# A Flamingo block with routed experts on one core: chunk sizes in another order, GpSimd's indirect DMAs released by other products and one at a time, and DVE's work moved between its maxima

## What is computed

```python
Q = split(layernorm(x) @ wq.T); K = split(ctx @ wk.T); V = split(ctx @ wv.T)
attn = softmax(einsum('bhqd,bhkd->bhqk', Q, K) / sqrt(8))
x = x + tanh(g_xattn) * merge(attn @ V)
y = layernorm(x)
logits = y @ Wr + br                       # 8 experts
topv, topi = top_k(logits, 2)
gates = softmax(where(chosen, logits, -inf))
h = relu(einsum('btd,edh->bteh', y, W1) + b1)
out = einsum('bte,bteh,ehd->btd', gates, h, W2) + einsum('bte,ed->btd', gates, b2)
x = x + tanh(g_ffn) * out
```

## Time and profile before

| | |
|---|---|
| median of 3 runs | 747.68 us (745.53 to 752.26) |
| the profiled execution's own time | 750.96 us |
| its span, first to last instruction | 749.2 us |
| PE busy with products | 601.1 us (80%) |
| DVE, ACT, POOL busy | 373.1, 368.3, 264.6 us |
| mean granted clock of TensorE | 0.88 of full speed |
| indirect DMAs issued by GpSimd | 112 scatters, 112 gathers |

### The profile page before, as it was taken

One profiled execution on the slowest core, in us unless ns is written; L12 is line 12 of the kernel. 1 busy time (PEld: TensorE's weight loads), 2 busy tenths in 40 slices (PEclk: granted clock), 3 DMA queues, 4 the chain that ended last, 5 costly groups with the idle time before them and its releaser, 6 DMA issues.

```text
span 749.2 us, 18488 instructions
## 1 busy us (share of the span) xinstructions
PE 601.1 (80%) x6213; PEld 430.1 (57%) x6213; DVE 373.1 (50%) x1361; ACT 368.3 (49%) x835; POOL 264.6 (35%) x281
## 2 busy tenths in 40 slices
PE   2459898868899887889989888988886679779467
PEld 0225555545566664556766557766455668667346
DVE  2446777765776445666544674454444032122044
ACT  5126755544566654456555555565553345344112
POOL 5020101045100345540444353444555661642720
PEclk9958988987999998799999889999798779999769
DMA  4445653554557524375644366632423435532211
GB/s 111 118 102 142 150 133 80 130 156 107 126 115 110 136 68 137 75 131 83 151 114 131 69 127 99 137 84 76 95 51 95 119 92 126 102 98 76 68 35 43
DMA packets 158121, 78.65 MB, mean 105 GB/s; under 512 B 85088, under 2 KB 153312, under 8 KB 158032
## 3 DMA queue, kind: packets, MB, share of 16 engines
q1 hardware_dynamic: 119760, 45.65, 28.6%
q10 hardware_dynamic: 31104, 17.13, 8.5%
q0 software_dynamic: 7168, 14.69, 7.6%
HBM read 30.72 MB, written 36.75 MB: 90 GB/s over the span
## 4 chain that ended last, share of the span: by engine, by line
PE 60%; issue 12%; DVE 10%; another core or an unknown queue 6%; ACT 6%; DMA 2%; ACTq 2%; SPq 1%; DVEq 0%
PE y L607 9%; PE scores L503 9%; PE bank_oT L517 9%; PE max_scores L482 5%; PE o L530 4%; PE hidden_p L593 3%; DVE neg_max L1025 3%; PE hidden_p L591 2%; ACT hidden L807 2%; PE max_scores L541 2%; PE bank_oT L647 2%; PE o L647 2%; PE hidden_p L592 2%; PE group L458 2%
## 5 line engine op out<-in xcount | busy, mean ns | idle before, releaser
L1025 DVE TENSOR_REDUCE neg_max<-max_scores 128x4 f32<-128x308 f32 x244 | 116.2, 476 | 177.6 <-PE max_scores L482 166.0
L741 ACT ACTIVATE probs<-scores 77x512 f32<-77x512 f32 x256 | 150.0, 596 | 88.5 <-PE scores L503 78.8
L1351 POOL DMA_INDIRECT back<-ys_dram,at x112 | 107.7, 961 | 110.3 <-PE scores L503 44.4
L1336 POOL DMA_INDIRECT xs_dram<-rows,at x112 | 109.5, 977 | 103.7 <-PE scores L503 75.3
L517 PE MATMUL bank_oT<-probs,v_cols 77*9 77x128 f32 x2048 | 112.2, 296 | 11.4 <-issue 6.3
L503 PE MATMUL scores<-q_st,k_st 128*77 128x128 bf16 x1024 | 115.3, 242 | 1.5 <-issue 1.3
L482 PE MATMUL max_scores<-k_st,q_st 128*128 128x308 bf16 x244 | 80.5, 330 | 41.0 <-DVE neg_max L1025 22.7
L503 PEld LDWEIGHTS scores<-q_st,k_st 128*77 128x77 bf16 x1024 | 79.3, 127 | 53.6 <-issue 46.1
L607 PE MATMUL y<-w_sb,hidden 128*128 x608 | 101.7, 314 | 0.0
L807 ACT ACTIVATE hidden<-hidden_p,b_cols 128x128 f32<-128x128 f32 x260 | 74.4, 370 | 50.3 <-PE hidden_p L593 40.8
L607 PEld LDWEIGHTS y<-w_sb,hidden 128*128 128x128 f32 x608 | 91.4, 216 | 3.3
(11 more groups left out here) (144 smaller groups left out, 943.3 us busy)
## 6 DMA issues: line engine op xcount, KB each, us to landing
ys_dram<-ys ACTq DMA_DIRECT2D x38, 256.0 KB
q_st<-q_dram SPq DMA_DIRECT2D x16, 512.0 KB
k_st<-k_dram SPq DMA_DIRECT2D x64, 77.0 KB
xs_all<-x SPq DMA_DIRECT2D x16, 256.0 KB, 3.9
q_dram<-q_hl SPq DMA_DIRECT2D x16, 256.0 KB
xs_dram<-zeros_b ACTq DMA_DIRECT2D x16, 256.0 KB, 3.2
out<-xs_all SPq DMA_DIRECT2D x16, 256.0 KB
k_dram<-k_hl SPq DMA_DIRECT2D x48, 77.0 KB
```

The lines of the kernel that those rows point to most:

```text
L741: nc.scalar.activation(probs[h][:], score_bank[h % 2][0:KEYS, :], ACT.Exp, scale=SCALE).then_inc(s_exp, 1)
L1025: V.tensor_reduce(neg_max[:, i // 2, :, h, i % 2], max_to(b, h)[:, 0:PER * KEYS].rearrange("p (j k) -> p j k", j=PER), AXIS_X, ALU.max, ne ...
L1336: G.indirect_dma_start(out=xs_dram[c % 2], out_offset=bass.IndirectOffsetOnAxis(ap=at[k][c % 4][:, i:i + 1], axis=0), in_=rows[c % 2][:, i ...
L1351: G.indirect_dma_start(out=back[k][:, b % 16, :], out_offset=None, in_=ys_dram[c % 2][0:TILES[c] * 128, :], in_offset=bass.IndirectOffsetO ...
```

## The change

The chunks become 12, 12, 12, 12, 8 sequences. At most two sequences a slot are scattered or gathered everywhere. `rows_out` is cut in two halves of two tiles, each waiting for its own half of `relu`; the second half stands behind the third product for the maxima. GpSimd's waits follow the products for the maxima while these exist, and after slot 78 every indirect DMA has a wait of its own. DVE's program takes the first maximum ahead of `normed1`, does `normed2` after the second, and adds the experts' outputs half before and half after the fourth. The gates have five buffers in place of four.

```diff
-CHUNKS = (8, 12, 12, 12, 12)
+CHUNKS = (12, 12, 12, 12, 8)
...
-        for _ in range(3 if late else 2):
+        for _ in range(2):
...
-            def rows_out(q):
-                pe.wait_ge(s_relu, 2 * q + 2)
-                if q:
+            def rows_out(q, half):
+                pe.wait_ge(s_relu, 2 * q + half + 1)
+                if half == 0 and q:
                     pe.wait_ge(s_ys, q)
-                if ranks_before(QUAD_AT[q] + 1):
+                if half == 0 and ranks_before(QUAD_AT[q] + 1):
                     pe.wait_ge(s_place, ranks_before(QUAD_AT[q] + 1))
-                for t in range(4):
+                for t in range(2 * half, 2 * half + 2):
...
-                last.then_inc(p_y, 1)
-                del held[q]
+                if half:
+                    last.then_inc(p_y, 1)
+                    del held[q]
...
                 for q in quads_at(t - 1):
-                    rows_out(q)
+                    rows_out(q, 0)
                 if active(sc):
                     values(sc, 0)
                     scores(sc, 2)
                 if active(mx):
                     max_scores(mx, 2)
+                for q in quads_at(t - 1):
+                    rows_out(q, 1)
...
+                sums = [b for b in range(SB) if SUM_AT[b] == t]
+                if active(mx):
+                    head_max(mx, 0)
                 if r == 1 and group_on(u - 1):
                     normed1(u - 1)
-                if r == 3 and group_on(u - 4):
-                    normed2(u - 4)
-                if active(mx):
-                    head_max(mx, 0)
...
                 if active(mx):
                     head_max(mx, 1)
+                if r == 3 and group_on(u - 4):
+                    normed2(u - 4)
...
-                for b in range(SB):
-                    if SUM_AT[b] == t:
-                        add_experts(b)
+                for b in sums[:(len(sums) + 1) // 2]:
+                    add_experts(b)
                 for n in dense_at(t - 1):
                     dense_add(n)
                 if active(mx):
                     head_max(mx, 3)
+                for b in sums[(len(sums) + 1) // 2:]:
+                    add_experts(b)
...
             def keep_pace(t, n, k):
+                if active(t - MAX_LAG):
+                    pool.wait_ge(p_max, HG * (t - MAX_LAG) + 2 * n + k)
+                    return
                 if t < LAST_ATT:
                     pool.wait_ge(p_st, clip(HG * (t - SCORE_LAG) + 2 * n + k, HG * B))
-                elif k == 0:
+                    return
+                if quads_at(t):
                     if n == 0:
-                        pool.wait_ge(p_hid, 2 * quads_before(t))
-                    if n == 1:
-                        pool.wait_ge(p_hid, 2 * quads_before(t) + len(quads_at(t)))
-                    if n >= 2:
+                        pool.wait_ge(p_hid, 2 * quads_before(t) + k)
+                    elif k == 0:
                         pool.wait_ge(p_y, quads_before(t))
-                    if dense_before(t):
-                        pool.wait_ge(p_dhid, HC * dense_before(t))
+                    else:
+                        pool.wait_ge(p_hid, 2 * quads_before(t) + 2)
+                if dense_at(t):
+                    if n == 0:
+                        pool.wait_ge(p_dhid, HC * dense_before(t) + k)
+                    elif k == 0:
+                        pool.wait_ge(p_dhid, HC * dense_before(t) + HC)
+                    elif dense_at(t - 1):
+                        pool.wait_ge(p_dy, dense_before(t))
```

More of the change, by code:

```diff
@@ L180, in flamingo_kernel @@
         gap_inv = sb("gap_inv", [128, NMAX])
-        gate = [[sb(f"gate{k}_{i}", [128, NMAX]) for i in range(4)] for k in range(2)]
+        gate = [[sb(f"gate{k}_{i}", [128, NMAX]) for i in range(5)] for k in range(2)]
         gate_all = sb("gate_all", [128, DENSE, E])
@@ L1104, in make_gates @@
                 n, r = SIZES[c], ROUTE * c + (BOTH if c < NC else CHOSEN)
-                first, second = gate[0][c % 4][:, 0:n], gate[1][c % 4][:, 0:n]
+                first, second = gate[0][c % 5][:, 0:n], gate[1][c % 5][:, 0:n]
                 dve.wait_ge(s_gexp, c + 1)
@@ L1110, in make_gates @@
                 dve.wait_ge(s_rt, r + 2)
-                if c >= 4:
-                    dve.wait_ge(s_sum, SEQ0[c - 3])
+                if c >= 5:
+                    dve.wait_ge(s_sum, SEQ0[c - 4])
                 V.tensor_scalar(first, gap_inv[:, 0:n], tanh_g[:, 1:2], None, ALU.mult).then_inc(s_rt, 1)
@@ L1117, in gates_of_all @@
             def gates_of_all():
-                first, second = (gate[k][NC % 4][:, 0:DENSE].unsqueeze(2).to_broadcast([128, DENSE, E]) for k in range(2))
+                first, second = (gate[k][NC % 5][:, 0:DENSE].unsqueeze(2).to_broadcast([128, DENSE, E]) for k in range(2))
                 dve.wait_ge(s_rt, ROUTE * NC + CHOSEN + 4)
@@ L1201, in add_experts @@
                 dve.wait_ge(s_rt, ROUTE * c + GATED)
-                V.scalar_tensor_tensor(out=to, in0=back[0][:, b % 16, :], scalar=gate[0][c % 4][:, i:i + 1], in1=to,
+                V.scalar_tensor_tensor(out=to, in0=back[0][:, b % 16, :], scalar=gate[0][c % 5][:, i:i + 1], in1=to,
                                        op0=ALU.mult, op1=ALU.add).then_inc(s_half, 1)
                 dve.wait_ge(s_half, b + 1)
-                V.scalar_tensor_tensor(out=to, in0=back[1][:, b % 16, :], scalar=gate[1][c % 4][:, i:i + 1], in1=to,
+                V.scalar_tensor_tensor(out=to, in0=back[1][:, b % 16, :], scalar=gate[1][c % 5][:, i:i + 1], in1=to,
                                        op0=ALU.mult, op1=ALU.add).then_inc(s_sum, 1)
```

## The result

The changed kernel takes 694.16 us (median of 6 runs, 686.74 to 698.42) against 749.97 us before: ratio 0.9225, 95% interval 0.9149 to 0.9302.

What follows compares the result with a forecast made beforehand. PE's own work plus waits from signals late beside GpSimd's indirect DMAs was taken to bound the kernel. Terms -8 - 5 - 4 - 15 + 3 + 2 = -27 us gave 724 against the profiled 750.96, median 721; range 704 to 743.

Steps and rivals of the forecast that it cites:

- The reading of slot 46: Attention, slot 46: DVE's reduction starts 1.16 us late because signals arrive late while GpSimd issues an indirect DMA and shortly after.
- I take the cost beside a quad as nothing: Attention slots with a quad: indirect DMAs cost nothing, since slot 54 with four is 0.2 us longer than slot 52 without.
- The second half of `rows_out`: Attention: moving it delays ACT's outputs and exponentials, perhaps `p_y` by 0.5 us; 0 to 10 us over 24 slots, +3 taken.
- the slower rival: Attention's quads: PE waits on ACT behind `p_y`, up to 1.5 us each, +36 in place of +3, 754 us; chance 0.14.
- Behind attention: Slots 78 on: 109 us plus 80 DMAs at 0.6 us gives 157 in place of 172, -15; ends 145 and 181.
- the 109 us without DMAs: From slot 78 on in the new kernel: time of 14 quads and the dense units before any DMA cost is added.
- Waits for the maxima in place of scores: GpSimd's pace in attention: each DMA moves by some 0.3 us; between -4 and +4 us, taken as nothing.
- Order of DVE: Attention: new order of `normed1` and `normed2` removes PE's waits at r = 3 and shortens those at r = 1; -8 us.
- Where DMAs fall in attention: Slots without a quad: 15 with DMAs in place of 18, at 1.8 us a slot, 0.45 us a DMA; -5 us.
- Quads: One quad leaves attention and returns behind it: a slot of 9.8 us becomes one of 5.7; -4 us in attention.
- A new meeting point: Slot 88: ACT's `store_y` of quad 32 needs chunk 2's gathers, issued until slot 87's end; 0 to 4 us, +2 taken.
- the rival built on it: Spacing of DMAs is worth nothing: still 0.76 us a DMA behind attention, no saving by fewer slots; 738 us, chance 0.24.

## Why the prediction was wrong

It had the sign, the two stretches and the effect (signals late beside GpSimd's DMAs) right, and half of the size in each stretch. In the profiled executions 55 us are gone: 28 ahead of slot 78, where the terms gave 14, and 27 from there on, where they gave 13. Its steps in their order:

- *The reading of slot 46*: of the 1.16 us that the reduction came late, DVE was busy with other work for the first 0.35 and idle for 0.81. The effect is as read; the 0.81 is its size there.
- *"I take the cost beside a quad as nothing"*: **this step failed first.** It rested on one pair of slots, 52 and 54. Slot 55, next to them, took 11.9 us at a clock of 0.86, and the mean of the 18 slots with DMAs was 10.35, that of the 6 without 9.33: 1.0 us a slot. One wait of GpSimd took 21.5 us off the kernel before. The change shortened these slots to 9.47, 18 us in 21 of them, for which the sum had no term.
- *The second half of `rows_out`*, +3 with 0 to 10: **wrong in sign**, -17 to -19 by undoing it, and this is how the change won most of those 18 us. I asked who waits for the moved products and not what their place does to the distance of the products that release GpSimd. 1.93 us in place of 0.87 between the third and fourth maxima keeps a DMA off the hidden part's signal. ACT's wait for `p_y`, on which the slower rival stood, cost nothing that shows: with the whole of `rows_out` late, where `p_y` is later still, the time was 693.55.
- *The clock*: the forecast had no term for it in slots with a quad. There it rose from 0.93 to 1.00, and most of what these slots gained is products that ran faster.
- *Behind attention*, -15 with ends of 145 and 181: 145.2 us, the better end, by (145.2 - 109) / 80 = 0.45 us a DMA where 0.6 was taken. The lower value had been read from attention's slots, where DMAs have pauses. The price isn't one number: the same 80 DMAs cost 22 us more at six a slot and 12 more with the old waits, and leaving 32 out saved 0.61 each. The clock rose with them, 0.87 to 0.94. The wait ahead of line 605 did vanish; the 109 us without DMAs no run tests.
- *Waits for the maxima in place of scores*, nothing: right, 695.02.
- *Order of DVE*, -8: 3 to 5 us by time, some 10 us by the waits; right in place, perhaps a little large.
- *Where DMAs fall in attention*, -5: leaving gathers out gave 0.45 us a DMA as well; what the new places alone are worth was not separated.
- *Quads*: one moved behind attention, as counted.
- *A new meeting point*, +2: the starts of ACT's outputs around slot 88 (606.7, 613.3, 620.6, 626.4) show no stall. It cost nothing that shows.
- The rule that a DMA never contends with a compute engine (the Trainium skill, SBUF — State Buffer, Who interferes with whom): the trace agrees as far as an instruction's own length goes. In the kernel before, 106 of DVE's reductions overlap an indirect DMA and take 477 ns on average, the other 138 take 476. But the rival built on it, 738 us, lay on the wrong side of the forecast: spacing these DMAs was worth tens of microseconds, through signals.

The single undoings add up to 19 + 12 + 5 + 16 + 22 = 74 us, more than 56, so they overlap. Old chunks, six a slot and old waits each leave longer or more trains behind attention than the changed kernel's two of eight (one of 10 beside two of eight; one of 12; four of eight), which may be what they share; no run tests that.

## What to carry to other kernels

Where one engine issues indirect DMAs beside a tight chain of others, look at what signal falls in the microsecond and a half from each issue (0.56 us late on average here, and up to 2.17), and let the issue wait for the one that PE's next step hangs on: one wait was worth 3% here and moved no work. Spread such DMAs evenly rather than in trains: behind trains of eight to 24 DVE had stood idle for 7 to 19 us here. And price an effect over all slots of a kind (the mean of 18), not over the pair that looks cleanest; when products are moved, ask also what they release.

## What the runs showed that was not expected

During a train of GpSimd's indirect DMAs, 1.26 us apart, few signals between engines pass, and after it DVE, ACT and GpSimd go on together: 1.8 us behind a train of eight, 2.4 us behind twelve. In the kernel before, the last of 24 in a row was issued from 717.25 to 718.20 us, and then:

```profile
722.26 1.12 DVE L1142 SCALAR_TENSOR_TENSOR xs_all<-bank_oT,gate_all,xs_all 128x128 f32<-128x128 f32 x4 [18.62 <-remote]
722.32 1.27 ACT L854 ACTIVATE q_st<-scores,b_cols 128x512 f32<-128x512 f32 x2 [13.46 <-remote]
```

4.1 us behind it, after 18.6 us of DVE's idle time. What holds the signals the runs don't show. That DVE's reductions and ACT's exponentials take as long beside an indirect DMA as without one (477 and 476 ns, 596 and 596) speaks for the signals' path and against the engines' own work.
